# First eight-by-eight attention: all sixteen products on VectorE in two buffers, none on GpSimd

## What is computed

```python
def _mha(x, Wqkv, bqkv, Wo, bo):
    S, B, _ = x.shape                       # 8 positions, 256 places
    qkv = x @ Wqkv.T + bqkv
    ...                                     # q, k, v: 4 heads of 32, to (place, head, position, 32)
    scores = jnp.einsum('bhqd,bhkd->bhqk', q, k) * (1.0 / np.sqrt(hd))
    att = jax.nn.softmax(scores, axis=-1)
    o = jnp.einsum('bhqk,bhkd->bhqd', att, v)
    return o.transpose(...).reshape(S, B, D) @ Wo.T + bo
```

## Time and profile before

| | us |
|---|---|
| median of 3 runs | 1127.69 (1127.55 to 1128.14) |
| the profiled execution | 1128.29 |
| its span, first to last instruction | 1126.6 |
| VectorE busy | 710.5 (63%) |
| TensorE busy | 728.4 (65%) |
| GpSimd busy | 121.5 (11%) |
| mean granted TensorE clock | 0.777 of full speed |

### The profile page before, as it was taken

How to read it: one execution, slowest core, us unless ns; L and a number is a source line. 1 busy time by engine, 2 the same in 40 slices (tenths; PEclk the granted TensorE clock), 3 DMA queues, 4 the chain that set the end, 5 groups by cost and what they waited for, 6 DMA issues and landing times. The chain is left out here.

```text
span 1126.6 us, 15348 instructions
## 1 busy us (share of the span) xinstructions
PE 728.4 (65%) x5634; PEld 604.3 (54%) x5634; DVE 710.5 (63%) x1459; ACT 370.0 (33%) x692; POOL 121.5 (11%) x86
## 2 busy tenths in 40 slices
PE   4976869970972620232990057999999962638994
PEld 2435869860642420232670055888888862436773
DVE  3139999549486799662344834377777657367465
ACT  2335234210441110100232621555555531234462
POOL 0011111000000178205005000000000002000000
PEclk9997567865986755655896555899999996868987
DMA  6000500041000100001111020000000000000000
GB/s 171 7 0 1 129 1 1 2 174 46 1 0 0 58 0 0 1 0 47 56 37 44 1 106 0 2 2 2 0 0 2 1 1 1 1 0 1 1 0 37
DMA packets 27865, 26.30 MB, mean 23 GB/s; under 512 B 17312, under 2 KB 26272, under 8 KB 27040
## 3 DMA queue, kind: packets, MB, share of 16 engines
q1 hardware_dynamic: 26784, 23.43, 6.8%
q0 software_dynamic: 1024, 2.10, 0.7%
HBM read 20.31 MB, written 5.21 MB: 23 GB/s over the span
## 5 line engine op out<-in xcount | busy, mean ns | idle before, releaser
L1748 PE MATMUL PS<-VXT,PT 128*128 128x73 f32 (+1 forms) x1024 | 126.6, 277 | 4.0 <-ACT PT L1771 4.0
L1748 PEld LDWEIGHTS PS<-VXT,PT 128*128 128x128 f32 x1024 | 119.6, 192 | 16.3 <-issue 12.2
L1858 DVE TENSOR_REDUCE MX<-PS 128x2 f32<-128x512 f32 x128 | 81.5, 684 | 47.2 <-PE PS L1713 46.7
L1771 ACT ACTIVATE PT<-PS 128x512 f32<-128x512 f32 x128 | 68.6, 596 | 47.3 <-PE PS L1718 47.3
L1710 PE MATMUL PS<-Q,KZ 32*128 32x256 f32 x512 | 78.6, 405 | 1.9 <-ACT KZ L1527 1.9
L1713 PE MATMUL PS<-KZ,Q 32*128 32x256 f32 x512 | 76.6, 438 | 5.0 <-DVEq L116 3.2
L281 PE MATMUL PS<-PB,NRM 128*128 128x128 f32 x80 | 17.9, 418 | 80.9 <-DVE NRM L265 45.3
L281 PEld LDWEIGHTS PS<-PB,NRM 128*128 128x128 f32 x80 | 16.5, 228 | 81.7 <-DVE NRM L1040 36.0
L1718 PE MATMUL PS<-MR,SEL 32*128 32x256 f32 x256 | 60.1, 472 | 0.0
L1713 PEld LDWEIGHTS PS<-KZ,Q 32*128 32x128 f32 x512 | 48.0, 205 | 8.5 <-ACTq L116 3.9
L290 ACT ACTIVATE TR<-PS 128x512 f32<-128x512 f32 x32 | 19.1, 598 | 97.8 <-PE PS L281 97.7
(11 more groups left out here) (389 smaller groups left out, 1978.7 us busy)
## 6 DMA issues: line engine op xcount, KB each, us to landing
PB<-in_pb SPq DMA_DIRECT2D x1, 5016.0 KB, 16.3
PB<-in_pd SPq DMA_DIRECT2D x1, 2888.0 KB, 9.6
X<-in_x SPq DMA_DIRECT2D x2, 1024.0 KB, 4.8
X<-fir_rows SPq DMA_DIRECT2D x2, 1024.0 KB, 6.6
TR<-fir_rows SPq DMA_DIRECT2D x2, 1024.0 KB, 8.7
PA<-in_pa SPq DMA_DIRECT2D x1, 1731.0 KB, 8.5
PC<-in_pc SPq DMA_DIRECT2D x1, 1560.0 KB, 6.9
by_expert<-PA SPq DMA_DIRECT2D x1, 1472.0 KB, 10.3
```

The costliest lines, as they stand in the source:

```text
L1748: last = nc.tensor.matmul(PS[:, UM.bank(n), col:col + VX], PT[:, k % 4, c, f * P:(f + 1) * P], v, start=(c == 0), stop=(c == 1))
L1771: nc.scalar.activation(PT[:, k % 4, :, :], PS[:, UM.bank(n), :].rearrange("p (c q) -> p c q", c=2), ACT.Exp).then_inc(c_act, 1)
L1858: nc.vector.tensor_reduce(MX[:, :, k], PS[:, UP_.bank(n), :].rearrange("p (f q) -> p f q", f=2), AX.X, ALU.max, negate=True).then_inc(p_dv ...
```

## The change

GpSimd makes no products any more. VectorE makes all sixteen. The buffer `PR` goes; the two buffers `PRP` are used in turn by VectorE alone. In each stage the first product is issued and waited for. Then for each step the next step's product is issued into the other buffer (counted, not waited for), behind it the current step's sum, and VectorE waits once, for both, before the next pair. The semaphores `products`, `summed` and `b_probs` go. The sizes and access patterns of all products and sums are as before.

```diff
-            PR = sbuf(sba, "PR", [P, 64, DK])
             PRP = sbuf(sba, "PRP", [P, 2, 64, DK])
             SC = sbuf(sba, "SC", [P, 2, NH, B, B])
-            products, summed, b_probs = sem("products"), sem("summed"), sem("b_probs")
...
-                    done = 0
-                    for stage in range(2):
-                        if stage == 0:
-                            pool.wait_ge(b_qkv_out, NT)
-                        else:
-                            pool.wait_ge(b_probs, 1)
-                        for f, h in STEPS[1::2]:
-                            if done >= 2:
-                                pool.wait_ge(summed, done - 1)
-                            (score_products if stage == 0 else value_products)(
-                                nc.gpsimd, f, h, PRP[:, done % 2, :, :]).then_inc(products, 1)
-                            done += 1
                     pool.wait_ge(r_place, 1)
...
-                    done = 0
+                    V.link(score_products(nc.vector, 0, 0, PRP[:, 0, :, :]))
                     for n, (f, h) in enumerate(STEPS):
                         to = SC[:, f, h, :, :].rearrange("p q k -> p (q k)")
-                        if n % 2 == 0:
-                            V.link(score_products(nc.vector, f, h, PR[:, :, :]))
-                            V.link(nc.vector.tensor_reduce(to, PR[:, :, :], AX.X, ALU.add))
-                        else:
-                            done += 1
-                            dve.wait_ge(products, done)
-                            nc.vector.tensor_reduce(to, PRP[:, (done - 1) % 2, :, :], AX.X, ALU.add)\
-                                .then_inc(summed, 1)
-                    dve.wait_ge(summed, done)
+                        if n + 1 < len(STEPS):
+                            V.mark(score_products(nc.vector, *STEPS[n + 1], PRP[:, (n + 1) % 2, :, :]))
+                        V.link(nc.vector.tensor_reduce(to, PRP[:, n % 2, :, :], AX.X, ALU.add))
...
-                    V.mark(nc.vector.tensor_tensor(scores, scores, bcast(SR[:, :], B), ALU.mult))
-                    dve.wait_ge(dve_step, V.done)
-                    dve.sem_inc(b_probs, 1)
+                    V.link(nc.vector.tensor_tensor(scores, scores, bcast(SR[:, :], B), ALU.mult))
+                    V.link(value_products(nc.vector, 0, 0, PRP[:, 0, :, :]))
                     for n, (f, h) in enumerate(STEPS):
                         to = OB[:, f:NT:2, h * DK:(h + 1) * DK]
-                        if n % 2 == 0:
-                            V.link(value_products(nc.vector, f, h, PR[:, :, :]))
-                            V.link(nc.vector.tensor_reduce(to, by_batch(PR[:, :, :]), AX.X, ALU.add))
-                        else:
-                            done += 1
-                            dve.wait_ge(products, done)
-                            last = nc.vector.tensor_reduce(to, by_batch(PRP[:, (done - 1) % 2, :, :]), AX.X, ALU.add)
-                            if n < len(STEPS) - 1:
-                                last.then_inc(summed, 1)
+                        if n + 1 < len(STEPS):
+                            V.mark(value_products(nc.vector, *STEPS[n + 1], PRP[:, (n + 1) % 2, :, :]))
+                        last = nc.vector.tensor_reduce(to, by_batch(PRP[:, n % 2, :, :]), AX.X, ALU.add)
+                        if n + 1 < len(STEPS):
+                            V.link(last)
                     v_ready(last)
```

## The result

Over 20 runs of each, the median is 1142.24 us against 1128.03 us for the kernel before; the ratio is 1.0119 with a 95% interval of 1.0097 to 1.0141. The kernel is slower by 1.2%, clear of the 0.2% that the prediction took as its limit. The profiled execution took 1140.75 us with a span of 1139.0 us, 12.4 us over the span before.

A forecast was written before the change was run, and what follows sets the result against it. The score and value stages, some 76 us, were taken as a chain on VectorE that TensorE waits for. 4.79 - 0.12 + 8.15 = +12.8 us gave 1140.5 us, range 1137.5 to 1145.0.

The forecast's parts named there:

- Score stage: Attention scores: 8 products and 8 sums all on VectorE, 36.36 us instead of 31.57, +4.79 us.
- Hand-over: Between softmax and value stage: the wait through b_probs, 0.15 us, becomes a plain wait of 0.035, -0.12 us.
- Value stage: Probabilities times v: 8 products and 8 sums all on VectorE, 47.92 us instead of 39.77, +8.15 us.
- d: A VectorE value product's own time without waiting; taken as 3.73 us, between bounds of 2.29 and 4.21.
- the turns: Value product time read by assuming VectorE's and GpSimd's products exclude each other: 3.62 and 3.63 us.
- L1839 scaled: Value product time estimated from another stepped-read instruction, 1.797 ns per element plus 161 ns fixed: 3.84 us.
- GpSimd's turn: Value stage: time each GpSimd product holds VectorE's products out, some 4.6 us, beside sums of 2.29 us.
- Rival 1: Value stage: the 4.21 us span is the product's own time; +16.7 us in all, 1144.3 us; chance 0.20.
- Rival 2: Value stage: stepped read is free, product 2.29 us; +1.3 us in all, 1129.0 us; chance 0.06.
- Rival 3: Both stages: issuing ahead saves nothing; +1.5 us on the forecast, 1142.0 us; chance within the forecast's 0.64.
- Behind it: After the value stage: TensorE turns OB and multiplies at clock 0.50 as before; costed at nothing.
- Rival 4: Later stages shift with TensorE's clock, 2 us either way, 1138.5 to 1142.5; chance 0.10, shared with other effects behind.

The follow-up runs named there:

- e1: Kernel before with only the score stage changed (all its products on VectorE), the value stage divided as before; ratio to the kernel before 1.0209.
- e3: Changed kernel with v copied by ScalarE so that the key position is contiguous in the value products; ratio to the kernel before 1.0164.
- e4: Kernel before, products still divided between the engines, with v copied by ScalarE so the key position is contiguous; ratio to the kernel before 1.0083.
- e10: e4 with 33 unused TensorE matmuls beside the value stage; ratio to the kernel before 0.9972, median of twelve runs 1135.56 us.
- e14: e10 with 31 more unused TensorE matmuls through the last norms of the experts' block; ratio to the kernel before 0.9994, median 1132.36 us.
- e8: Changed kernel with 40 unused TensorE matmuls from the start of the value stage; ratio to the kernel before 1.0132.

## Why the prediction was right

It said 1140.5 us with a range of 1137.5 to 1145.0; the median is 1142.24. It said a growth of 12.8 us; the medians grew by 14.2. The profiled execution was to have a span of 1139.4 and has 1139.0.

- Score stage: forecast +4.79, measured +4.70. The product with no GpSimd beside it was in the rows, and so were both kinds of joint; the overlap is 0.08 us, not 0.07.
- Hand-over: forecast and measured -0.12.
- Value stage: forecast +8.15, measured +7.12. The mechanism was right and one size was off: d was set at 3.73, between the turns (3.62) and L1839 scaled (3.84), and is 3.62. The reading of the turns, from two unlike spans, was exact. The scaled row came from an instruction with another step, and at 1.80 ns an element it was dearer than (3620 - 161)/2048 = 1.69 ns here. Taking the mean of a measurement of the thing itself and of an analogue cost 0.9 of the 1.0 us by which this term is off. GpSimd's turn, put there at some 4.6 us, was 8.82 - 3.62 = 5.20 us, of which 4.6 ran beside sums and 0.6 kept VectorE waiting; the sum did not use it.
- Rival 1 (4.21 us is the product's own) fell: 3.62 in after with GpSimd idle and in e1 where VectorE came first, 4.21 only beside GpSimd. Rival 2 (the step is free) fell by e3, where taking the step away gives 2.29. The formula of the Trainium skill for an fp32 tensor_tensor add, page "VectorE: DVE Perf Modes", section on the TRN2 errata, gives 2.29 us too and holds for the contiguous product to 2 ns. For the stepped read it is 1.33 us short, and the measurement decides. Rival 3 was priced at 1.5 us for overlaps that don't come; taking them away cost 1.8.
- Behind it: "I cost it at nothing" was wrong in detail. The prediction had both the turning and the product with wo at a granted clock of 0.50; before's product ran at 1.00 already, so there was something to lose. The stretch to the residual addition grew by 2.2 us, and later stretches gave 0.3 back net, among them +1.8 at the bias products of the experts and -2.2 at the product with wv. Rival 4 had this as up to 2 us either way. It is the right kind and, for other kernels of this study, far too small: 10 and 18 us occur. L281 on OB started at 477.66 us, not near 480. That the forecast came out within 0.4 us of the span owes something to chance: 1.1 us too much in the stages against 0.7 us that the rest added.

## What to carry to other kernels

Before moving work between GpSimd and VectorE, split each span into the instruction's own time and its wait for the other engine. Products with two SBUF inputs took turns here while sums ran on beside GpSimd, so GpSimd's share was worth having as long as VectorE had sums to make meanwhile; giving it up cost the two stages 11.8 us, though issuing ahead on an engine that works in order had won back 1.8. A constant span is no proof of an undisturbed instruction. And a gain of 8 us in one stage did not show in the total of e4, while the same code at another clock took 10 or 18 us longer elsewhere, so compare the stage before the total.

## What the runs showed of the hardware

- TensorE's granted clock is a cost of 10 to 18 us in stretches that the code leaves alone. The second attention took 243.3 us in before, where the clock rose 20 us after its first score maximum, and 261.1 in e1 and e10, where it rose after 60. In e14 it rose after 20, fell late in the stretch, and the stretch took 261.6.
- Work that keeps TensorE at 2.4 GHz up to the moment of need speeds up 16 turnings of 128x128 from 3.65 to 1.97 us; the same matmuls ending 10.5 us earlier gain next to nothing (3.68 us, and 10.2 against 10.6 for the whole stretch).
- A VectorE product with a step of 3072 bytes took 3.69 us beside unused matmuls and 3.68 beside memsets, against 3.62 alone. Here are the value product of e8 (stepped) and a product of e10 (contiguous), both beside those matmuls; the second has its plain 2.28 us.

```profile
L1087 DVE TENSOR_TENSOR PRP<-SC,QKV x8: 3624/3694/3706, 429.2 to 468.5; 128x2048 f32<-128x2048 f32 x8
```

```profile
438.09 2.28 DVE L1091 TENSOR_TENSOR PR<-SC,VB 128x2048 f32<-128x2048 f32 x1
```
